# A vision tower's four experts: the encoder's steps reordered, and GpSimd adds the two halves of the squares ahead of one variance matmul

## The reference

```python
def _ln(x, g, b):
    m = x.mean(-1, keepdims=True)
    v = ((x - m) ** 2).mean(-1, keepdims=True)
    return (x - m) * lax.rsqrt(v + EPS) * g + b
...
h = _ln(jax.nn.relu(x @ ew1 + eb1) @ ew2 + eb2, eg, ebeta)   # x: 4160 x 128, ew1: 128 x 256, ew2: 256 x 256
qkv = h @ aiw + aib
```

## Time and profile before

| what | value |
|---|---|
| time, median of 3 runs | 4191.71 us (4190.49 to 4195.33) |
| the profiled execution's own time | 4191.02 us |
| its span, first to last instruction | 4189.3 us |
| mean granted TensorE clock over the span | 0.944 of full |
| TensorE busy | 3695.9 us, 88% |
| VectorE busy | 2841.8 us, 68% |
| ScalarE busy | 2150.3 us, 51% |
| GpSimd busy | 1278.5 us, 31% |
| encoder of expert 1, first matmul to last `h` | 849.3 to 931.0 us |

### The profile page before, as it was taken

The page is one execution under the profiler, slowest core; times in us unless marked ns, Lnnn a source line. Parts: engine busy times, 40 slices in busy tenths (PEclk is TensorE's granted clock), DMA queues, the critical chain, the costliest instruction groups (busy, mean ns, idle before and its releaser), DMA issues. The chain is left out here.

```text
span 4189.3 us, 98294 instructions
## 1 busy us (share of the span) xinstructions
PE 3695.9 (88%) x36068; PEld 2265.2 (54%) x36068; DVE 2841.8 (68%) x5015; ACT 2150.3 (51%) x4378; POOL 1278.5 (31%) x1076
## 2 busy tenths in 40 slices
PE   5869689979988998952999999999999959999998
PEld 4645346646655655631555555555555527666665
DVE  8966568858858857876666666666666664555555
ACT  4536437737746755755444444444444445555554
POOL 0027537627726736744000000000000003444443
PEclk8889899989999999975999999999999978999999
DMA  8910100010010011025111111111111131111111
GB/s 174 176 33 0 52 18 2 1 56 2 0 42 16 0 42 32 0 87 157 46 50 48 45 48 50 48 44 48 49 49 43 49 103 52 54 53 53 53 53 30
DMA packets 392895, 205.07 MB, mean 49 GB/s; under 512 B 151221, under 2 KB 386474, under 8 KB 392106
## 3 DMA queue, kind: packets, MB, share of 16 engines
q1 hardware_dynamic: 392354, 203.09, 18.9%
q10 hardware_dynamic: 392, 0.03, 0.0%
HBM read 145.55 MB, written 57.51 MB: 48 GB/s over the span
## 5 line engine op out<-in xcount | busy, mean ns | idle before, releaser
L1827 PE MATMUL banks<-l_w,l_xs 128*64 128x512 f16 x6240 | 722.3, 381 | 15.0 <-DVE l_xs L1875 14.2
L1827 PE MATMUL banks<-l_w,l_hs 128*64 128x512 f16 x6144 | 705.8, 379 | 1.7 <-DVE l_hs L1881 1.7
L1827 PEld LDWEIGHTS banks<-l_w,l_xs 128*64 128x64 f16 x6240 | 344.6, 110 | 330.7 <-issue 25.6
L1827 PEld LDWEIGHTS banks<-l_w,l_hs 128*64 128x64 f16 x6144 | 348.3, 110 | 316.7 <-DVE l_hs L1881 2.2
L194 POOL MEMSET h_ident<- 128x128 f32 x1 | 0.2, 204 | 1444.3 <-POOLq L81 1444.3
L985 POOL TENSOR_TENSOR ax_p<-ax_p,ax_ri 128x520 f32<-128x520 f32 (+1 forms) x256 | 320.0, 1251 | 267.4 <-DVE ax_ri L1185 267.4
L1932 DVE SCALAR_TENSOR_TENSOR l_gates<-banks,l_unscale,l_bias 128x1024 f32<-128x1024 f32 x260 | 333.8, 1284 | 96.1 <-PE banks L1827 94.7
L1988 ACT ACTIVATE l_gates<-l_gates 128x768 f32<-128x768 f32 x260 | 219.1, 843 | 347.4 <-DVE l_gates L1932 347.4
L2259 PE MATMUL banks<-h_mem,h_w 128*128 128x320 f16 x2496 | 357.9, 300 | 1.0 <-DMA h_mem<-mem_scratch 1.0
L2554 ACT ACTIVATE h_work<-banks,h_bias,h_factor 128x320 f32<-128x320 f32 x312 | 192.3, 616 | 262.8 <-PE banks L2259 259.1
L2259 PEld LDWEIGHTS banks<-h_mem,h_w 128*128 128x128 f16 x2496 | 244.4, 98 | 94.9 <-issue 1.6
(11 more groups left out here) (306 smaller groups left out, 7180.4 us busy)
## 6 DMA issues: line engine op xcount, KB each, us to landing
image<-in_x_dram SPq DMA_DIRECT2D x192, 196.0 KB
l_x<-x_scratch SPq DMA_DIRECT2D x130, 256.0 KB, 3.0
mem_scratch<-l_hs SPq DMA_DIRECT2D x520, 64.0 KB, 1.9
h_mem<-mem_scratch SPq DMA_DIRECT2D x104, 320.0 KB, 3.7
x_scratch<-x_out SPq DMA_DIRECT2D x4, 4160.0 KB, 16.4
raw_in<-in_L_ffn_attn_in_w_dram SPq DMA_DIRECT2D x4, 768.0 KB, 4.5
h_scratch<-x_out SPq DMA_DIRECT2D x1, 2080.0 KB, 6.5
z_scratch<-z SPq DMA_DIRECT2D x1, 2080.0 KB, 11.6
```

Of the source, the lines that this page charges most:

```text
L1827: mm = pe.matmul(ps[d * HALF:(d + 1) * HALF, 2 * z + n, :], lhsT, w_of[e][:, d, kk, b, n * 512:(n + 1) * 512], start=(kk == 0 and turn_ == ...
```

## The change

Five edits in `experts_stage` and the attention it calls:

- GpSimd gets an instruction per step: it adds the second half of the squares of block k - 1 to the first, ahead of the multiplication for block k - 2. A new semaphore `halved` counts these.
- TensorE's variance is one matmul on that sum instead of two, waits for `halved`, and stands ahead of `w2` times block k - 1 instead of behind it.
- On VectorE the reciprocal of block k - 2 stands ahead of the bias additions of block k - 1; on ScalarE the Sqrt of block k - 2 stands ahead of the Square of block k - 1.
- `begin` stands after step 11, behind the last variance; `low_half`, `begin_first`, `dve_split` and `raise_weights` come one step earlier; `begin_second` after step 11.
- ScalarE copies the first unit's keys at the end of its encoder queue, and GpSimd masks them ahead of the class queries. TensorE waits for `first_kept` before it writes bank 7 again.

```diff
+        mask_keys(base, 0, 0, base * GROUP)
         pool.wait_ge(self.first_kept, BASE + 2 * e + 1)
         mask_class(0, base * GROUP)
-        mask_keys(base, 0, 0, base * GROUP)
...
+                    if u == 0:
+                        pe.wait_ge(self.first_kept, BASE + 2 * e + 2)
...
-        self.act_keys(act, ps[:, 6, :], factor, base, 0)
...
+                    if live(1):
+                        pool.wait_ge(squared, BASE + e * STEPS + k)
+                        pool.tensor_tensor(sq[:, 1 - par, 0], sq[:, 1 - par, 0], sq[:, 1 - par, 1], ALU.add).then_inc(halved, 1)
...
+                    if live(2):
+                        pe.wait_ge(halved, BASE + at - 1)
+                        pe.wait_ge(rooted, BASE + at - 2)
+                        pe.matmul(ps[:, 4, 0:WIDE], mean[:, :], sq[:, par, 0, :], start=True, stop=True).then_inc(varied, 1)
                     if live(1):
...
-                    if live(2):
-                        pe.wait_ge(squared, BASE + at - 1)
-                        pe.wait_ge(rooted, BASE + at - 2)
-                        for kk in range(KD):
-                            mm = pe.matmul(ps[:, 4, 0:WIDE], mean[:, :], sq[:, par, kk, :],
-                                           start=(kk == 0), stop=(kk == KD - 1))
-                        mm.then_inc(varied, 1)
-                laid_steps(body, {0: sum_vectors, 2: sum_values, 3: turn_most, 4: share_most, WSTEPS: begin})
+                laid_steps(body, {0: sum_vectors, 2: sum_values, 3: turn_most, 4: share_most, WSTEPS + 1: begin})
...
-                between = {1: gain_weights, 2: measure, 3: reduce_most, 4: size, 6: lambda: low_half(0),
-                           7: lambda: low_half(1).then_inc(w_low, 1), 8: begin_first,
-                           9: lambda: att.dve_split(dve, e * att.UNITS, 0, e * att.UNITS * GROUP), WSTEPS: begin_second}
+                between = {1: gain_weights, 2: measure, 3: reduce_most, 4: size, 5: lambda: low_half(0),
+                           6: lambda: low_half(1).then_inc(w_low, 1), 7: begin_first,
+                           8: lambda: att.dve_split(dve, e * att.UNITS, 0, e * att.UNITS * GROUP), WSTEPS + 1: begin_second}
...
+                    if live(2):
+                        dve.wait_ge(rooted, BASE + at - 1)
+                        if live(4):
+                            dve.wait_ge(h_ready, BASE + at - 3)
+                        dve.reciprocal(rs[:, par, :], sd[:, par, :]).then_inc(inverted, 1)
                     if live(1):
...
-                    if live(2):
-                        dve.wait_ge(rooted, BASE + at - 1)
-                        if live(4):
-                            dve.wait_ge(h_ready, BASE + at - 3)
-                        dve.reciprocal(rs[:, par, :], sd[:, par, :]).then_inc(inverted, 1)
...
+                    if live(2):
+                        act.wait_ge(varied, BASE + at_ - 1)
+                        if live(4):
+                            act.wait_ge(inverted, BASE + at_ - 3)
+                        act.activation(sd[:, par, :], ps[:, 4, 0:WIDE], ACT.Sqrt, bias=eps[:, 0:1]).then_inc(rooted, 1)
                     if live(1):
...
-                    if live(2):
-                        act.wait_ge(varied, BASE + at_ - 1)
-                        if live(4):
-                            act.wait_ge(inverted, BASE + at_ - 3)
-                        act.activation(sd[:, par, :], ps[:, 4, 0:WIDE], ACT.Sqrt, bias=eps[:, 0:1]).then_inc(rooted, 1)
...
-                laid_steps(body, {5: raise_weights})
+                laid_steps(body, {4: raise_weights, WSTEPS + 1: lambda: att.act_keys(act, ps[:, 6, :], factor[:, 0:1], e * att.UNITS, 0)})
```

More of the change, by code:

```diff
@@ L1402, in experts_stage @@
                                                       sem("x_inverted"), sem("x_h_ready"))
+        halved = sem("x_halved")
         saved = shared.x_saved
```

## The result

The changed kernel takes 4247.44 us (median of 4 runs, 4241.35 to 4255.27) against 4191.16 for the kernel before on the same chip (4190.49 to 4195.33). The ratio is 1.0133, 95% interval 1.0115 to 1.0152: slower. The forecast was 4248, range 4221 to 4288. The profiled execution took 4241.35 us itself, span 4239.6, which is 50.3 us more than the span before; that is the sum the profile has to explain, and this execution is the fastest of the four.

A forecast was written before the change was run, and what follows sets the result against it. Before, VectorE and TensorE were both near their limit; after, a one-step ring through every engine was to bound the encoder. +47.1 us over four experts, +12.6 clock, -3.3 warm start: +56.4 on 4191.0, median 4248, range 4221 to 4288.

The forecast's parts named there:

- The ring: Encoder: the chain from one block's additions through every engine to the next block's additions closes in one step, 7.75 us.
- Work between the steps: VectorE's work between encoder steps hides in its wait; `dve_split` (0.5) and `raise_weights` (0.2) still show, 0.7 us per encoder.
- Rival 4: GpSimd's addition in the encoder held in every step, 0.5 x 36 = +18 or more: 4266 to 4290; chance 0.06.
- The clock: Variance in the ring slowed by TensorE's lower clock, half of 0.70 us per step taken: 0.35 x 36 = +12.6.
- Start and end: Per encoder, first reciprocal 3.20 us earlier and keys mask off the path, 1.02 gained; moving `begin` and `begin_second` costs nothing.
- The warm start of the attention: `begin` just ahead of the class tokens lets TensorE run them at a higher clock: -3.3 us in all.
- Rival 1: Encoder bound by TensorE at 4.9 us per step, the ring closing over two steps: 4133 us; chance 0.03.
- Rival 2: Encoder ring closes over two steps but pace stays at 6.05; only start and end gain, 4175, or nothing; chance 0.03.
- Rival 3: TensorE, slow most of the time, bounds the encoder at 9.8 us per step: 4278 to 4313; chance 0.08.

The follow-up runs named there:

- the good one: Changed kernel with the single variance matmul behind `w2` again and the reciprocal and `h` one step later, Sqrt still ahead of Square: 4155.73 us, ratio 0.9907.

## Why the forecast held, point by point

**The ring.** Right, and the main matter. The forecast was 7.75, the turn took 7.55. By link, forecast against measured: reciprocal to additions 2.67 and 2.67, additions to Square 1.24 and 1.14, Square to GpSimd 1.06 and 0.97, GpSimd's addition to the variance 1.22 and 1.12, variance to Sqrt 0.93 and 1.01, Sqrt to reciprocal 0.63 and 0.64. The handover from ScalarE to GpSimd is 0.07 and that from GpSimd to TensorE 0.06, where I took 0.16 for both. 36 times 0.2 is 7 us too much. GpSimd's price, taken from another stage at 1.06, was 1.06.

**Work between the steps.** 0.7 per expert was forecast, about 0.2 came (one interval of 7.72 in place of 7.55). That is the interval in which `raise_weights` holds Sqrt, as forecast. `dve_split` did not meet GpSimd's addition, whose mean is 1064 ns over ten; the 0.5 for it was not spent. Rival 4 is refuted for this kernel. What it fears shows where VectorE's work between the steps falls on GpSimd's: with everything one step later GpSimd's addition took 1.74 us at 903.98, beside a VectorE instruction that itself took 1.90.

**The clock.** 12.6 was forecast, as half of an unknown. Measured 11.8 by the added matmuls, and 284.18 - 36 x 7.55 - 0.7 = 11.7 by the account. The bounds were 0 and 25, so that the middle fitted owes something to luck. The way was in part the one given. The clock fell in three places of an encoder and stretched one interval each time: to 8.25 (variance to Sqrt 1.69 in place of 1.01), to 8.28 and to 9.05. The second is a term that the forecast left out, when it called the variance the only TensorE work in the ring. There the variance ran at the full clock and `w2` behind it did not:

```profile
912.41 4.65 PE L1518 MATMUL banks<-ring,w 128*128 128x416 f32 x8
```

It takes 2.96 at the full clock, so VectorE's second addition waits for it and Square starts 1.87 after the first addition in place of 1.14. The third has both.

**Start and end.** The first reciprocal 3.19 earlier (forecast 3.20). The last multiplication took 2.25 us in place of 1.93, which I had at nothing: +0.33 per expert. It is the price of moving `begin_second`, forecast at none: that instruction of VectorE (L1142, 0.63 us at 955.89) now runs beside the last multiplication, and in the kernel before it ran beside the last but one, which took 2.25 there. Class scores 0.92 nearer on average (forecast 1.02), but the keys' move alone gave 0.42 in the kernel before. The rest is the next point.

**The warm start of the attention.** -3.3 was forecast for the stretch from the last `h` on, and it came in one half and not in the other. TensorE's projection of the class tokens, in the kernel before and in the changed one:

```profile
931.76 1.46 PE L999 MATMUL banks<-ax_x,w_in 128*128 128x64 f16 x24 [6.22 <-DVE ax_x L1197]
```

```profile
959.91 0.90 PE L999 MATMUL banks<-ax_x,w_in 128*128 128x64 f16 x24 [4.07 <-DVE ax_x L1199]
```

The granted clock from the last `h` to the class scores was 0.50 in the first and 0.76 in the second. The way took 5.04 us with the keys' move alone and 4.45 to 4.74 in the changed kernel, 2.0 less over four experts. That `begin` just ahead is what kept the clock up isn't shown: with the added matmuls it stands in the same place, and the way took 4.89 to 5.04. Behind the class scores the sign was wrong, +2.2 over three attentions: the granted clock in the first 23.6 us was 0.83 in three of four experts, and 0.91 or 0.92 before. The two halves nearly cancel.

**What I left out.** The start of an encoder, first matmul to Square of block 0, took 15.6, 11.3, 11.8 and 15.6 us in the four experts, and 15.1 to 15.6 before. Windows of the changed kernel, at the start of expert 0 and of expert 1:

```profile
521.00:538.00 17.00, 16.54 (x47) 10.96 (x47) 4.82 (x18) 4.59 (x7) 3.74 (x16) 0.62 0.37 157
```

```profile
867.00:879.00 12.00, 11.99 (x46) 7.25 (x46) 3.84 (x12) 4.26 (x6) 0.00 (x0) 0.86 1.03 294
```

TensorE is the bound in both, with a granted clock of 0.62 in one and 0.86 in the other; the same 46 or 47 records take 16.5 and 12.0 us. The ten experiments show 11.5 to 16.5 in no pattern that follows their edits, and executions of the changed kernel lie between 4241 and 4255. I take it as chance; no run was made to find what decides it. They do not explain by themselves that the profiled execution shows +50.3 where the medians show +56.3. The second profile of the changed kernel (4246.74 us, near the median) has starts that are 6.3 us shorter than before as well, and a span +55.7; it has 2.7 more in the attentions, 0.9 more in the intervals, 0.9 more in the starts and 0.7 more ahead of and behind the experts. That the forecast, 4248, fell on the median, 4247.44, is thus partly luck. In that second profile the intervals cost 8 us less than forecast (the ring 7 too long, the between-step work 2 too much, the clock about right; the other way, the intervals before were taken as 54.46 in every expert and are 1.3 less over the four), and the starts 6.3 less; the attentions cost 8.2 more, the stretches ahead of and behind the experts 3.5, the last multiplication 1.3.

**The rivals.** Rival 1 (TensorE bound, faster) needed a chain over two steps. It did not come, but its idea was sound: with the chain over two steps the kernel takes 4156, TensorE works without pause at 4.89 us a step for 24 us, and VectorE, as full, is what holds it afterwards. Rival 2 has its test in the intervals: none was under 7.5. Rival 3 (slow TensorE as the bound) is refuted by the clock of 0.91 and by the idle time ahead of the variance. The reason given against it, that TensorE gets its clock back when it works without pause, is not borne out as it stands: in the window from 521 to 538 it was busy 16.54 of 17 us at 0.62.

## What to carry to other kernels

Before you reorder queues for the sake of one stall, follow one block round: from an instruction through every engine to the next block's instance of it, counting each queue that it stands in, and divide the sum by the number of steps in which the chain closes; the largest such quotient is the pace, unless one engine's own work per step is larger. An order that puts the consumer of a block ahead of the producer of the next one on the same engine shortens the chain's steps, and so it must be paid for by a step of lag, here on the reciprocal alone. Work taken off an engine shows only when that quotient is below the engine's work: the same addition on GpSimd was worth nothing in the old order and 12.5 us in the good one.

## What the runs showed of the hardware that was not expected

- Two added matmuls of no use per step (four records of 0.35 us, 1.4 us together) made the changed kernel 14 us faster (4246.88 to 4233.02), since the granted clock stayed at 1.00 for the 60 us looked at. In the changed kernel, with TensorE idle for 2.39 us ahead of the variance in the turn shown and 21.6 us in the ten, it fell three times in the ring of expert 1: 0.60 from 895 to 899 us, 0.72 from 912 to 918 and 0.66 from 943 to 948, with 0.98 to 1.00 in between.
- Handovers are short: 0.06 to 0.07 us between GpSimd and ScalarE or TensorE in the ring.
- A two-input instruction on VectorE took 1.63 us in place of 0.68 while GpSimd's multiplication and addition ran, and GpSimd's own addition 1.47 in place of 1.06: both sides lose.
- The same attention took 244.0 to 246.5 us from its class scores to the next expert, in step with the granted clock of its first 23.6 us (0.93 to 0.76), in kernels that do and do not change it.
